# Attention scores on two 64-row halves of the PE array, into two banks, with one query copy

## Chip, cores and metric

The kernel runs on one core of a Trainium2 chip. The metric is the device time of one execution in microseconds (us), as the median of several executions. PE is TensorE, DVE is VectorE, ACT is ScalarE, POOL is GpSimd, SP is SyncE.

## The reference

The input is one sequence of 2048 tokens with 128 features. A first block (a gated linear recurrence with layer norms) is followed by two layers of local attention and a gated feed-forward network. Of one layer the part that matters here is the attention: 8 heads of 64 features, windows of 64 tokens, each query looking at its own window and the one before.

```python
q, k, v = split(shift_token(x) @ wqkv)           # (8 heads, N, 64)
q, k = rotary_xpos(l2norm(q) * qs, l2norm(k) * ks)
bk, bv = look_around(bk), look_around(bv)        # this window and the one before
sim = einsum('bhwid,bhwjd->bhwij', bq, bk)       # 64 queries x 128 keys
sim = where((i < j) | (i > j + WINDOW) | (j == -1), -max, sim)
out = einsum('bhwij,bhwjd->bhwid', softmax(sim), bv)
x = x + out @ wo                                 # then the feed-forward part
```

## The kernel before

**Tiles and groups.** Both layers together are 32 tiles of 128 tokens (two windows each), four tiles to a group. Every engine has its own program, written as `body(G, layer)` over a group with four steps j = 0 to 3; a step works on several tiles at different stages. The order on each engine is written out by hand, and engines wait for each other by semaphores alone. A loop runs the middle groups of each layer.

**One step on PE**, in order: `project_qkv` of tile t (L544, L545, L548: nine products of 512 columns), `project_out` of tile t-4 (L639), `transpose_probs` of tile t-2 (L633), `transpose_qk` of tile t-1 (L604, eight records into two banks), `transpose_o` of tile t-3 (L611), `mix_values` of tile t-2 (L669), and `scores` of tile t-1 (L650 and L655). In the step j = 0 four transposes of the next group's inputs (L595) stand ahead of the scores. In the step j = 2 four transposes of the normalised attention output (L676) stand ahead of the scores, and the feed-forward part of the group before (L544, L545, L548 with `w1`, then L704) behind them. Its third product, L548, waits for `h2_lo`, which DVE writes at L1097 from what ACT wrote at L869.

**One tile on POOL**: the two rotary additions into `rot` (L502, L503), a table (L469), the norms (L479, and L481, a power), in the step j = 1 also the deviations of the group's norm (L486, L488), and the scaling of `rot` (L517). The first needs `kt_done`, the end of the transposes L604 of the tile before, since there is one `rot`; those transposes need `rot_scaled`, the end of L517. So POOL and PE form a loop through `rot`.

**One tile on ACT**: the exponentials (L819), the copy of v (L836), the squares (L840), `probs_t` (L844), then the query copies: heads 0, 2, 4, 6 lie on partitions 0 to 63 of the transposed bank and go to `q_even` (L851), heads 1, 3, 5, 7 on partitions 64 to 127 and go to `q_odd` (L852). The other halves of both tensors are zeros, written once by POOL. Then comes the key copy `k_t` (L856), which PE waits for ahead of the scores, and `o_t` (L861).

**Scores.** A half of the heads (four) goes to one PSUM bank. The mask is a product of a 128 x 128 identity in bf16 with a mask of 512 columns, and each head adds two products with 128 contraction rows (of which 64 meet zeros), 64 stationary columns and 128 moving columns, one for each window. DVE takes the negative maximum of each half (L1081), ACT the exponentials.

Of the kernel before, what the change touches and what calls it, by code (L numbers as in the profile page):

```python
# [11 lines left out]
ALU = mybir.AluOpType  # L12
# [3 lines left out]
P = 128  # L16
DIM = 128
N = 2048
HEADS, DH, WINDOW = 8, 64, 64
# [38 lines left out]
def constant_block():  # L58

    r, c = np.arange(P)[:, None], np.arange(P)[None, :]  # L60
    a = r % WINDOW
    band = (c >= a) & (c <= a + WINDOW)
    first = band & ((r >= WINDOW) | (c >= WINDOW))
    m = lambda ok: np.where(ok, 0.0, MASKED)
    return np.concatenate([np.eye(P), m(band), m(first)], axis=1).astype(np.float32)


def sandwich_kernel(nc, x, w_hg_t, w_out_t, wqkv, wo, ln_g, ln_b, w1, b1, w2, b2,
                    tables, head_scales, consts, out):
    ctx = ExitStack()  # L70
    with ctx:
# [68 lines left out]
        q_even = sb("q_even", [P, PAIRS, P])  # L140
        q_odd = sb("q_odd", [P, PAIRS, P])
# [79 lines left out]
        settled = {e.name: sem(f"settled_{e.name}") for e in (mybir.EngineType.SP, mybir.EngineType.DVE, mybir.EngineType.Pool)}  # L221
# [213 lines left out]
        def _(pool):  # L435
            pool.memset(zeros[:, :], 0.0).then_inc(zeros_ready, 1)
            pool.memset(q_even[:, :, :], 0.0).then_inc(init_done, 1)
            pool.memset(q_odd[:, :, :], 0.0).then_inc(init_done, 1)
# [51 lines left out]
            pool.wait_ge(init_done, 7)  # L490
# [49 lines left out]
        def _(pe):  # L540
# [102 lines left out]
            def scores(a, half):  # L643


                if half == 0 and a.slot == 0:
                    pe.wait_ge(k_carried, a.group + 1)
                need(pe, (pt_saved0, pt_saved1)[half], a.t)
                b = s_bank[half]
                pe.matmul(b[:, :], ident_bf[:, :], mask_bf[1 if a.first else 0][:, :], start=True, stop=True)  # L650
                for h in range(4 * half, 4 * half + 4):
                    q, col = (q_even, q_odd)[h % 2][:, h // 2, :], (h % 4) * P
                    keys = k_t[:, h // 2, a.slot * P:]
                    for low in (0, 64):
                        last = pe.matmul(b[low:low + 64, col:col + P], q[:, low:low + 64], keys[:, low:low + P],  # L655
                                         start=False, stop=True, skip_group_check=True)
                last.then_inc(s_done, 1)

            def mix_values(a):
# [6 lines left out]
                for h in range(HEADS):  # L666
                    cols = slice(h * DH, (h + 1) * DH)
                    for low, v in ((0, v_mid[a.slot]), (64, v_tok[a.slot])):
                        last = pe.matmul(o_bank[low:low + 64, cols], probs_t[:, h, low:low + 64], v[:, cols],  # L669
                                         start=True, stop=True)  # L670
# [38 lines left out]
            pe.wait_ge(init_done, 7)  # L709
# [6 lines left out]
            def body(G, layer):  # L716
# [4 lines left out]
                for j in range(GT):  # L721
# [17 lines left out]
                    if prev.valid:  # L739
                        pe.wait_ge(q_saved, 2 * (prev.t + 1))  # L740
                        pe.wait_ge(k_saved, prev.t + 1)
# [4 lines left out]
                    if prev.valid:  # L746
                        scores(prev, 0)
                        scores(prev, 1)
# [8 lines left out]
        def _(act):  # L757
# [65 lines left out]
            def body(G, layer):  # L823
                number = isinstance(G, int)
                for j in range(GT):
# [22 lines left out]
                    if prev.valid:  # L848
                        act.wait_ge(qt_done, prev.t + 1)
                        need(act, s_done, 2 * prev.t)  # L850
                        act.copy(q_even[0:64, :, :], qt_bank[0:64, :].rearrange("p (c t) -> p c t", c=PAIRS)).then_inc(q_saved, 1)  # L851
                        act.copy(q_odd[64:128, :, :], qt_bank[64:128, :].rearrange("p (c t) -> p c t", c=PAIRS)).then_inc(q_saved, 1)  # L852
# [27 lines left out]
        def _(dve):  # L880
# [206 lines left out]
            def divide_o(a):  # L1087
# [3 lines left out]
                dve.tensor_tensor(o_tok[:, :].rearrange("p (h d) -> p h d", h=HEADS),  # L1091
                                  o_bank[:, :].rearrange("p (h d) -> p h d", h=HEADS),
                                  inv_sum[:, :].unsqueeze(2).broadcast_to([P, HEADS, DH]), ALU.mult).then_inc(o_ready, 1)
# [115 lines left out]
```

## Time and profile before

| | |
|---|---|
| median of 3 runs | 498.43 us (496.94 to 498.90) |
| the profiled execution | 496.46 us, its span 494.70 us |
| PE busy | 393.1 us (79%) |
| PE weight loads busy | 320.7 us (65%) |
| DVE busy | 325.1 us (66%) |
| ACT busy | 309.8 us (63%) |
| POOL busy | 307.1 us (62%) |
| mean granted TensorE clock | 0.923 of full speed |

The span is the stretch from the first to the last instruction; 1.76 us of the execution's time lie around it. Busy shares are means over stages with different limits. Matmuls are pipelined, and their ends in the profile are modelled, so starts tell more than ends. An fp32 product shows as two records in the profile.

### The profile page before, as it was taken

To read this page: it belongs to the slowest core of one execution; us is meant where nothing else is said; L and a number is where in the kernel's file an instruction comes from. 1 tells how busy PE (TensorE), PEld (TensorE's weight loads), DVE (VectorE), ACT (ScalarE), POOL (GpSimd) and SP (SyncE) were. 2 spreads that over 40 slices of the span, in tenths; PEclk is the share of its full clock that TensorE was granted. 3 is DMA by queue.
4 is the path that set the end of the run, shared out by engine and by line. 5 is a ranking of instruction groups with operands and counts; after the bars stand their busy time and mean duration, and the time that the engine had idled before them with its cause. 6 is when DMAs were issued, how large, how long until landed. Compare 5 with 4: busy or idle time off the path is not lost.

```text
span 494.7 us, 11132 instructions
## 1 busy us (share of the span) xinstructions
PE 393.1 (79%) x3768; PEld 320.7 (65%) x3768; DVE 325.1 (66%) x739; ACT 309.8 (63%) x884; POOL 307.1 (62%) x249
## 2 busy tenths in 40 slices
PE   3540058899999999999999989998968999587552
PEld 1330036778787887788878878887857778475432
DVE  6888962757776767766766775777556766545433
ACT  2363065778787787786868877887736867465120
POOL 2016757789889488938893887579574893570021
PEclk9895575999999999999999999999997999799858
DMA  8400240411331052105112410422015111020100
GB/s 300 125 0 0 64 107 1 119 28 28 102 76 30 0 140 57 27 22 139 38 28 52 121 37 19 111 66 52 0 28 143 27 27 27 21 50 1 23 21 21
DMA packets 42398, 28.21 MB, mean 57 GB/s; under 512 B 21699, under 2 KB 36597, under 8 KB 42357
## 3 DMA queue, kind: packets, MB, share of 16 engines
q1 hardware_dynamic: 42357, 27.68, 21.5%
q8 instruction: 23, 0.38, 0.3%
q14 instruction: 18, 0.15, 0.1%
HBM read 13.51 MB, written 3.15 MB: 34 GB/s over the span
## 4 chain that ended last, share of the span: by engine, by line
PE 52%; POOL 22%; DVE 14%; issue 7%; ACT 3%; DMA 1%; POOLq 0%; SPq 0%; DVEq 0%; ACTq 0%
POOL rn L481 8%; PE upper L655 8%; PE bank L544 5%; POOL rot L517 5%; PE bank L548 4%; PE bank L704 4%; PE bank L545 4%; PE bank L669 4%; PE upper L639 4%; PE upper L633 4%; PE bank L604 3%; POOL rot L503 3%; PE upper L604 3%; PE upper L650 2%; POOL tab L469 2%
## 5 line engine op out<-in xcount | busy, mean ns | idle before, releaser
L819 ACT ACTIVATE probs<-upper,neg_max 128x128 f32<-128x128 f32 x256 | 90.4, 368 | 60.7 <-DVE neg_max L1081 60.7
L502 POOL TENSOR_TENSOR rot<-rot_cos,rot_sin 128x512 f32<-128x512 f32 x32 | 40.8, 1275 | 95.4 <-PE upper L604 89.0
L481 POOL TENSOR_TENSOR rn<-floored,minus_half 128x16 f32<-128x16 f32 x32 | 96.7, 3022 | 2.7
L1081 DVE TENSOR_REDUCE neg_max<-upper 128x4 f32<-128x512 f32 x64 | 43.2, 683 | 43.7 <-PE upper L655 43.7
L517 POOL TENSOR_TENSOR rot<-rot,rn 128x1024 f32<-128x1024 f32 x32 | 60.9, 1903 | 1.9
L544 PE MATMUL bank<-wqkv_hi,act_t_hi 128*128 128x512 f32 x96 | 42.8, 446 | 19.9 <-DVE o_tok L1091 12.2
L655 PE MATMUL upper<-k_t,q_even 128*64 128x128 f32 x512 | 54.0, 290 | 0.0
L819 ACT ACTIVATION_READ_ACCUMULATOR probs<-upper,neg_max 128x1 f32 x256 | 52.7, 206 | 0.0
L655 PE MATMUL upper<-k_t,q_odd 128*64 128x128 f32 x512 | 50.7, 277 | 0.0
L1035 DVE TENSOR_TENSOR rot_cos<-bank,tab 128x512 f32<-128x512 f32 x64 | 43.9, 685 | 5.9 <-PE bank L548 5.3
L1035 DVE TENSOR_TENSOR rot_sin<-bank,tab 128x512 f32<-128x512 f32 x64 | 43.5, 680 | 0.0
L1042 DVE TENSOR_REDUCE ss<-sq 128x16 f32<-128x1024 f32 x32 | 38.8, 1211 | 5.7 <-ACT sq L840 5.5
L840 ACT ACTIVATE sq<-bank 128x512 f32<-128x512 f32 x64 | 38.3, 604 | 5.0 <-DVE rot_sin L1035 3.5
L503 POOL TENSOR_TENSOR rot<-rot_cos,rot_sin 128x512 f32<-128x512 f32 x32 | 40.5, 1267 | 0.0
L655 PEld LDWEIGHTS upper<-k_t,q_even 128*64 128x64 f32 x512 | 29.4, 138 | 16.3 <-issue 16.3
L545 PE MATMUL bank<-wqkv_hi,act_t_lo 128*128 128x512 f32 x96 | 39.0, 407 | 0.0
L548 PE MATMUL bank<-wqkv_lo,act_t_hi 128*128 128x512 f32 x96 | 38.9, 406 | 0.0
L669 PE MATMUL bank<-v_mid,probs_t 128*64 128x64 f32 x512 | 36.6, 225 | 1.3 <-ACT probs_t L844 0.9
L544 PEld LDWEIGHTS bank<-wqkv_hi,act_t_hi 128*128 128x128 f32 x96 | 18.8, 195 | 28.9 <-issue 19.6
L639 PEld LDWEIGHTS upper<-wo_sb,o_t 128*128 128x128 f32 x256 | 35.0, 200 | 3.8 <-ACT o_t L861 0.9
L669 PEld LDWEIGHTS bank<-v_mid,probs_t 128*64 128x64 f32 x512 | 32.2, 138 | 6.9 <-issue 5.6
L669 PE MATMUL bank<-v_tok,probs_t 128*64 128x64 f32 x512 | 36.6, 225 | 0.0
(132 smaller groups left out, 970.0 us busy)
## 6 DMA issues: line engine op xcount, KB each, us to landing
v_mid<-v_tok SPq DMA_DIRECT2D x64, 128.0 KB, 2.3
tab_raw<-tables SPq DMA_DIRECT2D x8, 512.0 KB, 3.4
h_tok<-group_in SPq DMA_DIRECT2D x14, 128.0 KB, 3.6
x_res<-group_in SPq DMA_DIRECT2D x28, 64.0 KB, 1.8
wqkv_raw<-wqkv SPq DMA_DIRECT2D x2, 768.0 KB, 6.0
x_in<-x SPq DMA_DIRECT2D x4, 256.0 KB, 3.5
head_scale<-head_scales SPq DMA_DIRECT2D x8, 128.0 KB, 3.9
group_in<-normed SPq DMA_DIRECT2D x4, 256.0 KB
```

The costliest lines, as they stand in the source:

```text
L481: pool.tensor_tensor(rn[:, 0:2 * HEADS], floored[:, 0:2 * HEADS], minus_half[:, :], ALU.pow).then_inc(rn_ready, 1)
L503: pool.tensor_tensor(rot[:, :, 32:64], rot_cos[:, :, 32:64], rot_sin[:, :, 0:32], ALU.add).then_inc(rot_added, 1)
L517: pool.tensor_tensor(rot[:, :, :], rot[:, :, :], rn[:, 0:2 * HEADS].unsqueeze(2).broadcast_to([P, 2 * HEADS, DH]), ALU.mult).then_inc(rot_ ...
L544: pe.matmul(out_ap, lhs, rhs, start=True, stop=False)
L545: pe.matmul(out_ap, lhs_lo, rhs, start=False, stop=False)
L548: return pe.matmul(out_ap, lhs, rhs_lo, start=False, stop=True)
L639: last = pe.matmul(misc_bank[:, 0:DIM], o_t[:, c, :], wo_sb[a.layer][:, c, :], start=(c == 0), stop=(c == 3))
L655: last = pe.matmul(b[low:low + 64, col:col + P], q[:, low:low + 64], keys[:, low:low + P], start=False, stop=True, skip_group_check=True)
L669: last = pe.matmul(o_bank[low:low + 64, cols], probs_t[:, h, low:low + 64], v[:, cols], start=True, stop=True)
L819: last = act.activation(probs[:, h, :], s_bank[half][:, (h % 4) * P:(h % 4 + 1) * P], ACT.Exp, bias=neg_max[a.par][:, h:h + 1], accum_out= ...
L1035: dve.tensor_tensor(dst[:, n * HEADS:(n + 1) * HEADS, :], src, table.unsqueeze(1).broadcast_to([P, HEADS, DH]), ALU.mult).then_inc(done, 1)
L1081: dve.tensor_reduce(neg_max[a.par][:, 4 * half:4 * half + 4], src, AX.X, ALU.max, negate=True).then_inc(max_ready, 1)
```

## The change

Query and key of a head now meet on the 64 partitions on which the head already lies. There is one query tensor, `q_t`, filled by one copy of 128 partitions. Even heads use the array's rows 0 to 63 and write bank 0, odd heads use rows 64 to 127 and write bank 1. The mask comes as four products of a 64 x 64 identity in bf16 with 512 columns, in the same quarters as the scores, ahead of all scores; the mask for a layer's first tile is used for its first window alone. Both halves are issued interleaved in one call, which first waits for both copies out of the two banks, then increments a semaphore. The order of the heads in the two banks changes with it (0, 2, 4, 6 and 1, 3, 5, 7), and so do the columns in `mix_values` and in `divide_o`. Two memsets on POOL at the start fall away.

```diff
-    first = band & ((r >= WINDOW) | (c >= WINDOW))
+    first = band & (c >= WINDOW)
...
-        q_even = sb("q_even", [P, PAIRS, P])
-        q_odd = sb("q_odd", [P, PAIRS, P])
+        q_t = sb("q_t", [P, PAIRS, P])
...
-            pool.memset(q_even[:, :, :], 0.0).then_inc(init_done, 1)
-            pool.memset(q_odd[:, :, :], 0.0).then_inc(init_done, 1)
...
-            def scores(a, half):
-                if half == 0 and a.slot == 0:
+            def scores(a):
+                if a.slot == 0:
                     pe.wait_ge(k_carried, a.group + 1)
-                need(pe, (pt_saved0, pt_saved1)[half], a.t)
-                b = s_bank[half]
-                pe.matmul(b[:, :], ident_bf[:, :], mask_bf[1 if a.first else 0][:, :], start=True, stop=True)
-                for h in range(4 * half, 4 * half + 4):
-                    q, col = (q_even, q_odd)[h % 2][:, h // 2, :], (h % 4) * P
-                    keys = k_t[:, h // 2, a.slot * P:]
+                need(pe, pt_saved0, a.t)
+                need(pe, pt_saved1, a.t)
+                settle(pe)
+                for low in (0, 64):
+                    for half in range(2):
+                        rows = slice(64 * half, 64 * half + 64)
+                        pe.matmul(s_bank[half][low:low + 64, :], ident_bf[rows, rows],
+                                  mask_bf[1 if a.first and low == 0 else 0][rows, :], start=True, stop=True)
+                for p in range(PAIRS):
                     for low in (0, 64):
-                        last = pe.matmul(b[low:low + 64, col:col + P], q[:, low:low + 64], keys[:, low:low + P],
-                                         start=False, stop=True, skip_group_check=True)
-                last.then_inc(s_done, 1)
+                        for half in range(2):
+                            rows = slice(64 * half, 64 * half + 64)
+                            at = a.slot * P + low
+                            last = pe.matmul(s_bank[half][low:low + 64, p * P:(p + 1) * P], q_t[rows, p, low:low + 64],
+                                             k_t[rows, p, at:at + P], start=False, stop=True, skip_group_check=True)
+                            if p == PAIRS - 1 and low == 64:
+                                last.then_inc(s_done, 1)
...
                 for h in range(HEADS):
-                    cols = slice(h * DH, (h + 1) * DH)
+                    head = 2 * (h % PAIRS) + h // PAIRS
+                    cols = slice(head * DH, (head + 1) * DH)
...
-                        scores(prev, 0)
-                        scores(prev, 1)
+                        scores(prev)
...
-                        act.copy(q_even[0:64, :, :], qt_bank[0:64, :].rearrange("p (c t) -> p c t", c=PAIRS)).then_inc(q_saved, 1)
-                        act.copy(q_odd[64:128, :, :], qt_bank[64:128, :].rearrange("p (c t) -> p c t", c=PAIRS)).then_inc(q_saved, 1)
+                        act.copy(q_t[:, :, :], qt_bank[:, :].rearrange("p (c t) -> p c t", c=PAIRS)).then_inc(q_saved, 1)
...
-                dve.tensor_tensor(o_tok[:, :].rearrange("p (h d) -> p h d", h=HEADS),
-                                  o_bank[:, :].rearrange("p (h d) -> p h d", h=HEADS),
-                                  inv_sum[:, :].unsqueeze(2).broadcast_to([P, HEADS, DH]), ALU.mult).then_inc(o_ready, 1)
+                split = lambda ap: ap.rearrange("p (c f d) -> p f c d", f=2, d=DH)
+                inverse = inv_sum[:, :].rearrange("p (f c) -> p f c", f=2).unsqueeze(3).broadcast_to([P, 2, PAIRS, DH])
+                dve.tensor_tensor(split(o_tok[:, :]), split(o_bank[:, :]), inverse, ALU.mult).then_inc(o_ready, 1)
```

## Rows read from the trace of the kernel before

**Rows 1.** The page's first part: busy time, share of the span, instructions.
```profile
PE 393.1 (79%) x3768; PEld 320.7 (65%) x3768; DVE 325.1 (66%) x739; ACT 309.8 (63%) x884; POOL 307.1 (62%) x249
```
**Rows 2.** Waits over the span: waiting group, released by, us, times, longest.
```profile
POOL rot L502 <- PE upper L604: 89.0, 31, 7.6
```
**Rows 3.** Timeline of POOL: start, duration, instruction, idle time before with its releaser.
```profile
157.49 1.28 POOL L502 TENSOR_TENSOR rot<-rot_cos,rot_sin 128x512 f32<-128x512 f32 x1 [0.98 <-PE upper L604]
...
173.98 1.27 POOL L502 TENSOR_TENSOR rot<-rot_cos,rot_sin 128x512 f32<-128x512 f32 x1 [7.57 <-PE upper L604]
...
183.60 1.27 POOL L502 TENSOR_TENSOR rot<-rot_cos,rot_sin 128x512 f32<-128x512 f32 x1 [1.23 <-PE upper L604]
...
193.38 1.28 POOL L502 TENSOR_TENSOR rot<-rot_cos,rot_sin 128x512 f32<-128x512 f32 x1 [1.40 <-PE upper L604]
...
201.00 1.90 POOL L517 TENSOR_TENSOR rot<-rot,rn 128x1024 f32<-128x1024 f32 x1
...
204.22 1.28 POOL L502 TENSOR_TENSOR rot<-rot_cos,rot_sin 128x512 f32<-128x512 f32 x1 [0.98 <-PE upper L604]
```
**Rows 4.** Timeline of PE and ACT around the step j = 1.
```profile
193.60 0.27 PE L669 MATMUL bank<-v_mid,probs_t 128*64 128x64 f32 x1
...
194.50 0.58 ACT L856 COPY k_t<-upper 128x512 f32<-128x512 f32 x1
...
194.53 0.22 PE L669 MATMUL bank<-v_tok,probs_t 128*64 128x64 f32 x1
...
197.87 0.50 PE L544 MATMUL bank<-wqkv_hi,act_t_hi 128*128 128x512 f32 x1
...
200.93 1.04 PE L633 MATMUL upper<-const,probs 128*128 128x128 f32 x8
202.96 0.66 PE L604 MATMUL bank<-const,rot 128*128 128x128 f32 x4 [0.99 <-POOL rot L517]
```
**Rows 5.** Timeline of PE and DVE in the step j = 2.
```profile
206.01 0.38 PE L650 MATMUL upper<-mask_bf,ident_bf 128*128 128x512 bf16 x1
...
207.34 0.39 PE L650 MATMUL upper<-mask_bf,ident_bf 128*128 128x512 bf16 x1
...
207.69 0.69 DVE L1097 TENSOR_TENSOR h_lo<-h_t,h_hi 128x512 fp32r<-128x512 f32 x1 [2.73 <-ACT h_t L869]
...
208.15 0.39 PE L655 MATMUL upper<-k_t,q_even 128*64 128x128 f32 x4
...
208.37 0.39 PE L655 MATMUL upper<-k_t,q_odd 128*64 128x128 f32 x4
...
208.69 0.50 PE L544 MATMUL bank<-h_hi,w_hi 128*128 128x512 f32 x1
...
209.26 0.39 PE L548 MATMUL bank<-h_lo,w_hi 128*128 128x512 f32 x1
```
**Rows 6.** Timeline of POOL over the first tiles.
```profile
77.55 1.26 POOL L502 TENSOR_TENSOR rot<-rot_cos,rot_sin 128x512 f32<-128x512 f32 x1 [2.20 <-PE upper L604]
83.34 1.90 POOL L517 TENSOR_TENSOR rot<-rot,rn 128x1024 f32<-128x1024 f32 x1
88.08 1.28 POOL L502 TENSOR_TENSOR rot<-rot_cos,rot_sin 128x512 f32<-128x512 f32 x1 [2.84 <-PE upper L604]
...
117.44 1.27 POOL L502 TENSOR_TENSOR rot<-rot_cos,rot_sin 128x512 f32<-128x512 f32 x1 [0.98 <-PE upper L604]
```
**Rows 7.** Timeline of PE: restarts after idle time.
```profile
14.60 0.66 PE L554 MATMUL bank<-const,normed 128*128 128x128 f32 x4 [1.74 <-DVE normed L947]
...
75.41 1.12 PE L604 MATMUL bank<-const,rot 128*128 128x128 f32 x4 [4.28 <-POOL rot L517]
...
372.86 0.79 PE L544 MATMUL bank<-wqkv_hi,act_t_hi 128*128 128x512 f32 x1 [6.07 <-DVE o_tok L1091]
```
**Rows 8.** Windows: length, busy us by engine, granted clock, DMA share, GB/s.
```profile
16.00:18.00 2.00, 1.98 (x5) 1.46 (x6) 2.00 (x7) 0.00 (x0) 0.00 (x0) 0.54 0.57 127
18.00:20.00 2.00, 0.83 (x2) 0.11 (x1) 1.97 (x5) 0.00 (x0) 0.00 (x0) 0.60 0.49 116
```

More of the change, by code:

```diff
@@ L220, in sandwich_kernel @@
         dve_chain = sem("dve_chain")
-        settled = {e.name: sem(f"settled_{e.name}") for e in (mybir.EngineType.SP, mybir.EngineType.DVE, mybir.EngineType.Pool)}
+        settled = {e.name: sem(f"settled_{e.name}") for e in (mybir.EngineType.SP, mybir.EngineType.DVE, mybir.EngineType.Pool, mybir.EngineType.PE)}
         block = ctx.enter_context(nc.Block())
@@ L488, in deviation_roots @@
                 pool.tensor_tensor(rn[:, 2 * HEADS:], floored[:, 2 * HEADS:], minus_half[:, 0:GT], ALU.pow).then_inc(done, 1)
-            pool.wait_ge(init_done, 7)
+            pool.wait_ge(init_done, 5)
             def body(G, layer):
@@ L707, in feed_forward @@
                 last.then_inc(down_done, 1)
-            pe.wait_ge(init_done, 7)
+            pe.wait_ge(init_done, 5)
             pe.wait_ge(const_bf, 3)
@@ L739, in body @@
                     if prev.valid:
-                        pe.wait_ge(q_saved, 2 * (prev.t + 1))
+                        pe.wait_ge(q_saved, prev.t + 1)
                         pe.wait_ge(k_saved, prev.t + 1)
```

## Prediction

> **What bounds the kernel now.** I read the page first: PE leads with 79% of the span [rows 1], but no engine is near full, so a share does not say what PE time is worth. The waits say more: POOL's first addition L502 waits 31 times for the transposes L604, 89.0 us in all [rows 2]. That is the loop through the single `rot`: L604 of one tile frees it, POOL adds, takes the power and scales, L517 releases the next L604. So I laid POOL's timeline over a group, since the distance from one L502 to the next is the period of a step [rows 3]. The four are 16.49 us (157.49 to 173.98, the step with the feed-forward part), 9.62, 9.78 and 10.84 us. POOL idles 7.57 us ahead of the first and 1.23, 1.40 and 0.98 us ahead of the others.
>
> The idle 1.2 to 1.4 us is no slack. In the last of the steps L517 ends at 202.90 [rows 3], L604 starts at 202.96 [rows 4], and L502 follows at 204.22 [rows 3]: 1.32 us from scaling to addition are the eight transposes and the hand-overs. So POOL's loop, not PE's work, sets 9.62 and 10.84 us. PE is nearly as late in the two short steps and 0.99 us early in the last [rows 4]. Only the long step is PE's from end to end. Pattern and sizes repeat for six groups. The score work falls once into the long step, and three times into steps in which POOL sets the end.
>
> **The cost of a score call, before.** In the long step it runs from the first mask at 206.01 over the second at 207.34 to the product behind it at 208.69: 1.33 + 1.35 = 2.68 us [rows 5]. Four records (two pairs, both windows at once) are 0.22 us apart (208.15 to 208.37), so a half's sixteen take 0.88. A mask has 512 columns in one pass, as many as two such pairs: 0.22. What is left of 1.33, about 0.24, goes to the two changes between a full-array product and 64-column ones.
>
> **After.** The 16 logical products (32 records) remain. If the row halves overlap, eight slots of 0.11 give 0.88. The nearest row for the rate of issue is L669: 32 records of 64 columns start between 193.60 and 194.53 [rows 4], 0.030 us each, so 0.96 for 32. I take 0.93. The four masks overlap to 0.22 to 0.25. One change of mode in and one out, 0.12 each. Together 1.42 us, 1.26 less. If the row halves do not overlap, it is 0.44 + 1.76 + 0.24 = 2.44, only 0.24 less (the changes of mode saved); the trace of before has no product on half the rows, so both ends stay in the range. I take overlap, because the pairs of column halves, the nearest thing that the trace has, do overlap fully.
>
> The Trainium skill, "TensorEngine Tiling (Array Packing)", Theoretical Speedup and Key Properties, says that a contraction of 64 or less gains up to 2x from row tiling, and that a change of mode drains the array. By that rule the call is the 1.42 us above, without it 2.44. The gaps of 0.1 us at each change in this trace (208.37 + 0.22 to 208.69, [rows 5]) agree with the drain; on the row halves it shows nothing.
>
> The other parts: one query copy for two saves ACT one of about 0.58 us, by the same-sized k copy [rows 4]. In the steps j = 1 that moves `k_t` earlier: it ends at 195.08 while PE's last L669 started at 194.53, so PE gains up to 0.45 us there; the rest of ACT has cover. The strided `divide_o` has the same 512 elements per partition; I set it at nothing (DVE is off the path in all but two steps; if it doubled to 1.4 us it would show in those two, +1.4). The wait for both bank copies costs nothing, since `mix_values` has waited for both already; `settle` is a bare semaphore instruction, hidden by 0.4 us of spare below. Behind the scores PE queues the projection, and DVE and POOL wait for that, with 1 us or more to spare. The first maximum comes after both halves, but both end at 1.42 us, about when the first ended before (1.33). The memsets lie in the start-up, under input loads.
>
> **What of it counts.** (1) The long step, six times. With the scores 1.26 us shorter, L544 starts near 207.4 instead of 208.69. But its third product L548 needs `h_lo`, which DVE ends at 208.38 (207.69 + 0.69), and DVE had waited for ACT, which waited for the transposes ahead of the scores: none of that moves. So L548 goes from 209.26 to about 208.43: 0.83 us, and 0.43 is lost in a new wait [rows 5]. 6 x 0.83 = 5.0 us.
> (2) The first tiles, where PE and ACT are late and the half clock doubles the scores. POOL's loop caps this: from 77.55 a pass takes 7.69 (to the end of L517 at 85.24) plus 1.32, 9.0 us, twice, then 9.65 with the table, twice, which leads to 114.9 instead of 117.44 [rows 6]. PE's own saving there, over 5 us in four calls, is more than the cap. 2.5 us.
> (3) The steps j = 0, 9.78 us against the 9.62 of the pure loop [rows 3]: about 0.1, six times, 0.6 us.
> (4) All other steps: POOL or, in two of the second layer, DVE sets them: 0. The end: 0.
> Sum 8.1 us.
>
> **What it brings with it.** The time won in POOL's steps becomes PE idle time ahead of L604. In the steps j = 1 PE is ready near 201.8 and starts at 202.96. After, it is ready 1.26 + 0.45 = 1.7 us earlier: a gap of about 2.9 us. The granted clock falls to its lower level (1.2 GHz for 2.4) after such gaps in this trace: with idle of 4.28 and 6.07 us each time, and once, near 16 us [rows 8], after a gap of only 1.74 us and one short burst of transposes [rows 7]. The gaps of 1.0 us in six steps never cost it. 2.9 us lies between, so I give each of the six steps near one half. The price: the shortest low stretch with a busy PE is read from two windows, 2 x (1 - 0.54) x 2 + 2 x (1 - 0.60) x 2 = 3.4 us [rows 8], and half of the PE work in it is lost, 1.7 us; right behind this gap follows the long step, in which PE sets the time. With two or three of six: 4.2 us lost. Gaps in the other steps grow to 1.3 to 1.9 us, which I take to hold.
>
> **Forecast.** 8.1 - 4.2 = 3.9 us won. The profiled execution (496.46 us, 494.70 of span and 1.76 around it) would become 492.6; it lies 1.97 us under the median of the runs, 498.43, to which I apply the same difference: 494.5 us, chance 0.38 (two or three falls; own range 493 to 496.5).
>
> **The rivals.**
> - The clock holds, or falls once. For it: no gap under 1.5 us that stood between long busy stretches ever cost it. Against: the event near 16 us [rows 7, 8]. 498.43 - 8.1 = 490.3 (to 492 with one fall). Chance 0.28.
> - Slower by the clock: it falls in four to six steps, or stays low twice as long (as it did for over 5 us after the restart at 75.41). 6 x 1.7 = 10.2, or three at 3.4: 8.1 - 10.2 = +2.1, up to +5: 500.5 to 503; with four falls 497. It turns to a loss from the fifth fall on. Chance 0.16.
> - The row halves do not overlap. Call 2.44 us: 6 x 0.24 = 1.4, the first tiles still some 2.2 from the single copy and the half clock, gap in j = 1 only 1.7 us, so no falls: 3.6 won, 494.8. Chance 0.12.
> - Row halves cost: weight loads and products of the four quarters run one after another, 32 slots of 0.11 = 3.5 us, call 4.2 us. Then each long step is 1.5 longer (9 us) and PE, nearly as late as POOL already, sets the short ones too (some 1.1 in sixteen): +27, 525 us. It decides as soon as a call is longer than 2.68 us. Chance 0.06.
>
> A change of 0.5%, 2.5 us, is about what a measurement of this kernel can tell from none. Faster (under 495.9): 0.28 from the clock that holds, 0.28 of the 0.38, 0.09 of no overlap, 0.65 in all. Same: 0.10, 0.03 and 0.05 from the fourth and fifth fall, 0.18. Slower 0.17. For 8 in 10 the range goes from 490 to 500.5.
>
> **What would show it.** Right: 32 L655 records within about 1 us and four L650 within 0.3; in the long step a new wait of L548 for `h_lo` of some 0.4 us and a period of 15.7 us where the clock holds; the other periods still 9.6 and 10.8; PE idle ahead of L604 in j = 1 near 2.9 us; and dips of the clock right after some of them, with L604 or L669 at double spacing. Wrong: a period of 9.6 that shrinks (then POOL's loop was not the bound), scores as long as before, or a low clock after the 1.3 to 1.9 us gaps as well.

## The result and the profile after

The changed kernel takes 500.76 us (median of 14 runs, 498.48 to 502.21), the kernel before 497.93 us beside it (14 runs, 496.04 to 498.90). The ratio is 1.0061 with a 95% interval of 1.0043 to 1.0079: slower by 3 us. Predicted were 494.5 us, with a range of 490 to 500.5. The profiled execution took 499.41 us with a span of 497.6 us, against 496.46 and 494.70. The line numbers move by two to four in the new file: POOL's addition L499 was L502, L514 was L517; PE's L601 was L604, L630 was L633, L673 was L669, L680 was L676, L541 and L545 were L544 and L548, and L657 are the scores; DVE's L1099 was L1097, ACT's L871 was L869.

The first part of the page of the changed kernel, with the line of the granted clock in 40 slices; it answers to [rows 1]:

```profile
PE 363.8 (73%) x3832; PEld 297.8 (60%) x3832; DVE 329.9 (66%) x739; ACT 287.0 (58%) x852; POOL 304.0 (61%) x247
...
PEclk9995575999999999899989999998998989789957
```

PE has 29 us less to do than before and the kernel is slower. The second line has single eights in its long row of nines, where the kernel before had only nines: the clock falls in places where it held. The windows below show where. The mean granted clock is 0.904 of full speed, against 0.923.

The same wait as [rows 2], among the waits over the span: the bound is still POOL's loop with the transposes.

```profile
POOL rot L499 <- PE upper L601: 91.3, 31, 8.5
```

POOL's timeline over a little more than a group, which answers to [rows 3]:

```profile
155.82 1.28 POOL L499 TENSOR_TENSOR rot<-rot_cos,rot_sin 128x512 f32<-128x512 f32 x1 [0.98 <-PE upper L601]
...
171.58 1.28 POOL L499 TENSOR_TENSOR rot<-rot_cos,rot_sin 128x512 f32<-128x512 f32 x1 [6.85 <-PE upper L601]
...
181.21 1.28 POOL L499 TENSOR_TENSOR rot<-rot_cos,rot_sin 128x512 f32<-128x512 f32 x1 [1.23 <-PE upper L601]
...
190.94 1.28 POOL L499 TENSOR_TENSOR rot<-rot_cos,rot_sin 128x512 f32<-128x512 f32 x1 [1.32 <-PE upper L601]
...
202.63 1.26 POOL L499 TENSOR_TENSOR rot<-rot_cos,rot_sin 128x512 f32<-128x512 f32 x1 [1.80 <-PE upper L601]
...
219.18 1.29 POOL L499 TENSOR_TENSOR rot<-rot_cos,rot_sin 128x512 f32<-128x512 f32 x1 [8.14 <-PE upper L601]
```

The first long step is 15.76 us (155.82 to 171.58), and the short ones behind it 9.63 and 9.73 us. Then comes 11.69 us where 10.87 stood one group earlier, and a long step of 16.55 us. The pair 10.87 + 15.76 = 26.63 us is what the change gives (27.34 before), the pair 11.69 + 16.55 = 28.24 us what it becomes when the clock falls. One of the six pairs is of the first kind, five of the second.

PE's timeline over that second pair, with DVE's subtraction for `h_lo`; it answers to [rows 4, 5]:

```profile
196.90 1.04 PE L630 MATMUL upper<-const,probs 128*128 128x128 f32 x8
...
200.54 1.06 PE L601 MATMUL bank<-const,rot 128*128 128x128 f32 x4 [2.61 <-POOL rot L514]
201.40 1.06 PE L601 MATMUL upper<-const,rot 128*128 128x128 f32 x4
...
205.26 0.41 PE L650 MATMUL upper<-mask_bf,ident_bf 64*64 64x512 bf16 x4
205.50 1.04 PE L657 MATMUL upper<-k_t,q_t 64*64 64x128 f32 x32
206.48 0.50 PE L541 MATMUL bank<-h_hi,w_hi 128*128 128x512 f32 x1
...
206.86 0.69 DVE L1099 TENSOR_TENSOR h_lo<-h_t,h_hi 128x512 fp32r<-128x512 f32 x1 [4.31 <-ACT h_t L871]
...
207.60 0.50 PE L545 MATMUL bank<-h_lo,w_hi 128*128 128x512 f32 x1 [0.39 <-DVE h_lo L1099]
```

The score call runs from 205.26 to 206.48: 1.22 us for what took 2.68. Ahead of the first L601 PE idles 2.61 us, where it idled 0.99. The four records of that L601 take 0.86 us (200.54 to 201.40). Where the clock holds the same row looks like this (PE's timeline, 46 us earlier):

```profile
154.55 0.66 PE L601 MATMUL bank<-const,rot 128*128 128x128 f32 x4 [2.61 <-POOL rot L514]
155.04 0.60 PE L601 MATMUL upper<-const,rot 128*128 128x128 f32 x4
```

There they take 0.49 us, after the same gap of 2.61 us. The windows of the changed kernel (length, busy us by engine, granted clock, DMA share, GB/s) show the low level between 200.7 and 204, and once more near the end:

```profile
200.00:202.00 2.00, 1.46 (x7) 1.46 (x8) 2.00 (x5) 0.36 (x1) 0.83 (x2) 0.66 0.60 131
202.00:204.00 2.00, 2.00 (x21) 1.67 (x21) 0.55 (x1) 1.40 (x3) 1.37 (x2) 0.50 0.00 0
204.00:206.00 2.00, 2.00 (x52) 1.69 (x52) 0.00 (x0) 0.63 (x1) 2.00 (x3) 0.98 0.00 0
...
444.00:446.00 2.00, 2.00 (x27) 1.67 (x27) 0.00 (x0) 1.17 (x2) 0.00 (x0) 0.50 0.00 0
```

**Where 2.9 us of span went.** The table goes by the starts of POOL's L499 (L502 before), as [rows 3, 6] do; it begins with the second of the 32, at which rows 6 begin.

| stretch | before, us | after, us | difference |
|---|---|---|---|
| up to the second addition | 77.55 | 78.22 | +0.7 |
| first tiles, four periods | 39.89 | 37.58 | -2.3 |
| six long steps, each with the step ahead of it, clock held | 27.34 each | 26.63 each | -4.3 |
| falls of the clock in five of these pairs | 0 | 1.4 to 1.6 each | +7.8 |
| all other steps | | | -1.1 |
| behind the last addition | 60.74 | 62.88 | +2.1 |

The start varies by kernel and execution (77.4 to 79.4 us over the profiles of this case), so its 0.7 is not laid on the change. In the row of the other steps nearly all (1.0) comes from the two steps that DVE sets, 17.98 + 17.86 before and 17.52 + 17.31 after. Without filler in these steps their sum lies between 34.5 and 36.8 us over the profiles of this case, and at 34.9 in the kernel before with scores left out for slot 3 (below), so this 1.0 is not laid on the change either. The end: PE idles 0.78 us ahead of the last L601 (at 442.50), the clock falls, and the way to the second L630 of the next step is 1.4 us longer; the rest is a transfer 0.2 us later and a clock that comes back 0.5 us later in the last feed-forward part. The kernel before had no fall at that place.

### The profile page after: what moved, and what is told of

Its sections match the earlier page's. It is cut to its first block, busy times and chain, and to the rows that moved or that the text cites. A ratio compares the mean times of both kernels' runs of the same rounds, so it can differ in the third digit from the quotient of the medians.

```text
span 497.6 us, 11258 instructions
## 1 busy us (share of the span) xinstructions
PE 363.8 (73%) x3832; PEld 297.8 (60%) x3832; DVE 329.9 (66%) x739; ACT 287.0 (58%) x852; POOL 304.0 (61%) x247
## 4 chain that ended last, share of the span: by engine, by line
POOL 34%; PE 32%; DVE 16%; issue 12%; ACT 4%; DMA 1%; POOLq 1%; SPq 0%; DVEq 0%; ACTq 0%
POOL rn L478 14%; POOL rot L514 8%; POOL rot L500 6%; PE bank L708 4%; PE bank L601 4%; PE bank L545 3%; PE upper L601 3%; PE bank L673 3%; POOL tab L466 3%; PE bank L541 3%; PE bank L542 2%; PE upper L636 2%; DVE normed L949 2%; PE upper L608 2%; POOL rot L499 1%
## 5 line engine op out<-in xcount | busy, mean ns | idle before, releaser
L499 POOL TENSOR_TENSOR rot<-rot_cos,rot_sin 128x512 f32<-128x512 f32 x32 | 40.8, 1275 | 97.7 <-PE upper L601 91.3
L478 POOL TENSOR_TENSOR rn<-floored,minus_half 128x16 f32<-128x16 f32 x32 | 94.1, 2940 | 2.7
L541 PE MATMUL bank<-wqkv_hi,act_t_hi 128*128 128x512 f32 x96 | 44.3, 462 | 28.4 <-DVE o_tok L1095 16.0
L514 POOL TENSOR_TENSOR rot<-rot,rn 128x1024 f32<-128x1024 f32 x32 | 60.9, 1904 | 1.9
L601 PE MATMUL bank<-const,rot 128*128 128x128 f32 x128 | 22.5, 303 | 36.6 <-POOL rot L514 36.6
L541 PEld LDWEIGHTS bank<-wqkv_hi,act_t_hi 128*128 128x128 f32 x96 | 18.9, 197 | 43.2 <-issue 31.2
L601 PEld LDWEIGHTS bank<-const,rot 128*128 128x128 f32 x128 | 14.9, 149 | 42.5 <-POOL rot L514 40.3
L673 PE MATMUL bank<-v_mid,probs_t 128*64 128x64 f32 x512 | 39.4, 235 | 0.4 <-issue 0.4
L673 PE MATMUL bank<-v_tok,probs_t 128*64 128x64 f32 x512 | 39.5, 235 | 0.0
L545 PE MATMUL bank<-wqkv_lo,act_t_hi 128*128 128x512 f32 x96 | 39.3, 410 | 0.0
L673 PEld LDWEIGHTS bank<-v_mid,probs_t 128*64 128x64 f32 x512 | 35.1, 148 | 6.9 <-issue 6.7
L630 PE MATMUL upper<-const,probs 128*128 128x128 f32 x256 | 35.1, 278 | 4.9 <-ACT probs L822 4.7
L843 ACT ACTIVATE sq<-bank 128x512 f32<-128x512 f32 x64 | 36.7, 612 | 2.3 <-DVE rot_sin L1037 2.3
```

What stands on the lines that cost most here:

```text
L478: pool.tensor_tensor(rn[:, 0:2 * HEADS], floored[:, 0:2 * HEADS], minus_half[:, :], ALU.pow).then_inc(rn_ready, 1)
L499: pool.tensor_tensor(rot[:, :, 0:32], rot_cos[:, :, 0:32], rot_sin[:, :, 32:64], ALU.add).then_inc(rot_added, 1)
L514: pool.tensor_tensor(rot[:, :, :], rot[:, :, :], rn[:, 0:2 * HEADS].unsqueeze(2).broadcast_to([P, 2 * HEADS, DH]), ALU.mult).then_inc(rot_ ...
L541: pe.matmul(out_ap, lhs, rhs, start=True, stop=False)
L545: return pe.matmul(out_ap, lhs, rhs_lo, start=False, stop=True)
L601: last = pe.transpose(b[:, p * P:(p + 1) * P], rot[:, h:h + 2, :].rearrange("p h d -> p (h d)"), ident)
```

## The experiments

All ratios are to the kernel before, timed in the same batch (497.59, 497.56 and 498.02 us in the three). Three theories stood against each other: **A**, the idle gap of PE ahead of L601 costs the clock, and the falls cost more than the change gives; **B**, products on half the rows are themselves what the clock falls by; **C**, the loss has nothing to do with the clock (the joint wait for both banks, the late first maximum, the new wait for `h_lo`). The gap stands in PE's own step j = 2, the one with the L680 and the feed-forward part; the prediction called it j = 1, after POOL's number for the tile. That slip placed two of the first four kernels at a wrong step, and what they showed is told below.

**The changed kernel once more**, unchanged.

> The changed kernel itself, unchanged, once more. Theory A (gap and clock): the gaps of PE ahead of the qk transposes in the steps j = 1 are 2.6 us and each throws the clock to its lower level by chance, 1.7 us for each fall; the first profile had five falls in six such steps and one more near the end. A second profile should again show four to six of them, not always in the same steps, and a time of 499 to 502 us. Theory B (the half-row products themselves count as less work for the clock, wherever the gap): the same falls, also elsewhere.

Measured 500.12 us (499.90 to 502.39), 1.0065 (1.0048 to 1.0082). The gaps are again 2.60 to 2.62 us (the sixth 2.37), but the falls come in four of the six pairs instead of five, and three more stand elsewhere (one in the first tiles, two in the last steps). Near 16 us the clock is low for 13.7 us, where the kernel before has 3.4 and the first profile nothing. The total repeats, and a single fall does not: the same gap in the same code holds the clock in one group and loses it in the next. The spread of the changed kernel's runs (498.48 to 502.21) is of the size of two or three falls; that it comes from them is not shown, since the kernel before, with no fall in these pairs in its profile, spreads by 2.9 us.

**Filler in the wrong step.** Filler is work whose result nobody reads: eight bf16 products into a bank that the next transposes overwrite, ahead of L601.

```diff
+                        if j == 1:
+                            for _ in range(8):
+                                pe.matmul(kt_bank[:, :], ident_bf[:, :], mask_bf[0][:, :], start=True, stop=True)
                         transpose_qk(prev)
```

> The changed kernel with eight extra mask-shaped products (full array, bf16, 512 columns, 0.22 us each, 1.8 us in all) written into the free k bank ahead of the qk transposes in the steps j = 1; their result is overwritten. They fill the gap of 2.6 us down to 0.8. Theory A: no fall in those six steps, 5 x 1.7 = 8.5 us less than the changed kernel, near 492 us, 6 us under the kernel before; period of the step j = 1 back at 10.85 us and of the long step at 15.75. Theory B (half-row products starve the clock): part of the falls stay, in the long step behind the scores or in the steps j = 3. Rival C (the loss lies in something else, such as the new wait for h_lo): no change or slower by the extra work.

Measured 505.41 us, 1.0180 (1.0151 to 1.0208): a miss, near 492 was expected. PE's timeline of this kernel:

```profile
145.12 1.67 PE L740 MATMUL upper<-mask_bf,ident_bf 128*128 128x512 bf16 x7
...
146.63 0.60 PE L601 MATMUL bank<-const,rot 128*128 128x128 f32 x4
...
157.44 1.03 PE L601 MATMUL bank<-const,rot 128*128 128x128 f32 x4 [2.61 <-POOL rot L514]
```

and POOL's of the same kernel:

```profile
136.80 1.28 POOL L499 TENSOR_TENSOR rot<-rot_cos,rot_sin 128x512 f32<-128x512 f32 x1 [1.23 <-PE upper L601]
...
147.84 1.28 POOL L499 TENSOR_TENSOR rot<-rot_cos,rot_sin 128x512 f32<-128x512 f32 x1 [2.62 <-PE upper L601]
```

The filler (seven of its eight records are in the trace) fills a gap of 0.5 to 0.9 us with 1.7 us of work and delays L601, so POOL's period there is 11.04 us instead of 9.73 (10.36 to 11.04 over the six groups), and in all that adds 5.7 us. The gap of 2.61 us stands untouched in the next step, and three of the six pairs fall; behind the one shown L601 is slow. It tells nothing between A and B, but it gives the price of PE work in a step that POOL sets: nothing up to the gap, most of it beyond.

**The two row halves one after the other.**

```diff
-                for low in (0, 64):
-                    for half in range(2):
-                        rows = slice(64 * half, 64 * half + 64)
+                for half in range(2):
+                    rows = slice(64 * half, 64 * half + 64)
+                    for low in (0, 64):
                         pe.matmul(s_bank[half][low:low + 64, :], ident_bf[rows, rows], ...
-                for p in range(PAIRS):
-                    for low in (0, 64):
-                        for half in range(2):
+                    for p in range(PAIRS):
+                        for low in (0, 64):
```

> The changed kernel with the two row halves issued one after the other: mask and products of half 0, then of half 1; the same 36 products. A call should take 2.3 to 2.45 us instead of 1.22, so the gap in j = 1 shrinks from 2.6 to about 1.5 us. Theory A: no falls or one, the long step 15.75 to 16.3 us, the first tiles still 2 us faster, in all 494 to 495 us: faster than the changed kernel although its scores take twice as long. Theory B: the half-row products are still there and last longer, so the falls stay and the time is over 500 us.

Measured 498.69 us (495.99 to 501.02), 1.0019 (0.9999 to 1.0038): a miss for A, by which 494 to 495 was expected, and under what B said (over 500). It is no measurable difference to before, and with a longer score call it is faster than the changed kernel, whose interval lies above. PE's timeline of one score call:

```profile
159.31 0.40 PE L650 MATMUL upper<-mask_bf,ident_bf 64*64 64x512 bf16 x2
159.55 0.71 PE L655 MATMUL upper<-k_t,q_t 64*64 64x128 f32 x10
160.00 0.40 PE L650 MATMUL upper<-mask_bf,ident_bf 64*64 64x512 bf16 x2
160.09 1.18 PE L655 MATMUL upper<-k_t,q_t 64*64 64x128 f32 x22
161.20 0.50 PE L541 MATMUL bank<-h_hi,w_hi 128*128 128x512 f32 x1
```

The call takes 1.89 us (159.31 to 161.20), not 2.3 or more: half 1's masks start after ten of half 0's sixteen records, so the halves still overlap in part. The gap ahead of L601 shrinks to 2.30 to 2.32 us, yet five of six pairs fall. That profile is of the slowest of the kernel's twelve runs (501.02 us), so the usual number of falls may be smaller. The gap is not the 1.5 us for which A had been put to the test, so the run settles nothing about the clock. What it does show is that a clean long step is 15.78 us, no longer than with 1.22 us of scores, as L545 waits for `h_lo` in any case.

**Less score work in the kernel before, one step early.** Only the last head of each bank in the tiles of slot 2; three quarters of those scores are left out.

```diff
-                for h in range(4 * half, 4 * half + 4):
+                for h in range(4 * half + (3 if a.slot == 2 else 0), 4 * half + 4):
```

> The kernel before with less work: in the steps j = 0 the scores of only one head of four in each bank are computed (the other heads' scores are left out, so the output is not the reference's). All products are on the full 128 rows. That takes 1.3 us from PE once in a group and widens the gap in the step j = 1 from 1.0 to about 2.3 us. Theory A: the clock falls in some of the six steps, 1.7 us each, and the kernel gets slower by 3 to 9 us although it does less. Theory B: no fall, the time of the kernel before, 498 us.

Measured 497.68 us, 1.0004 (0.9992 to 1.0016), where A expected a loss of 3 to 9 us. That is no case against A, for the thinned scores stand one step ahead of the right place: the gap they widen is only 0.38 us, and the one of interest stays (PE's timeline of this kernel):

```profile
191.87 0.66 PE L604 MATMUL bank<-const,rot 128*128 128x128 f32 x4 [0.38 <-POOL rot L517]
...
202.71 0.66 PE L604 MATMUL bank<-const,rot 128*128 128x128 f32 x4 [1.07 <-POOL rot L517]
```

No pair falls, and the time does not move. As a control that holds: three quarters of the scores of eight tiles are worth nothing where POOL sets the step.

**Less score work in the kernel before, in the right step.** The same, for `a.slot == 3`. The products keep all 128 rows, so this is the gap without the half rows.

```diff
+                for h in range(4 * half + (3 if a.slot == 3 else 0), 4 * half + 4):
```

> The kernel before with less work at the right place: for the last tile of each group, whose scores PE computes right ahead of the step with the large gap, only one head of four in each bank is computed (the others' scores are left out, so the output is not the reference's). All products are on the full 128 rows; the gap grows from 1.0 to 2.3 us. Theory A: falls in three to five of the six long steps, 1.7 us each: 503 to 506 us, slower than the kernel before although it does less. Theory B: no falls, 498 us.

Measured 500.94 us (499.02 to 501.68), 1.0058 (1.0036 to 1.0081): the kernel before with work taken out is as slow as the changed kernel, though less slow than A expected (503 to 506). PE's timeline of this kernel:

```profile
157.69 1.12 PE L604 MATMUL bank<-const,rot 128*128 128x128 f32 x4 [2.29 <-POOL rot L517]
```

and POOL's of the same kernel:

```profile
148.12 1.27 POOL L502 TENSOR_TENSOR rot<-rot_cos,rot_sin 128x512 f32<-128x512 f32 x1 [1.40 <-PE upper L604]
...
159.84 1.26 POOL L502 TENSOR_TENSOR rot<-rot_cos,rot_sin 128x512 f32<-128x512 f32 x1 [1.86 <-PE upper L604]
...
177.01 1.27 POOL L502 TENSOR_TENSOR rot<-rot_cos,rot_sin 128x512 f32<-128x512 f32 x1 [8.77 <-PE upper L604]
```

The gap is 2.29 us here (2.29 to 2.41 over the six), and three pairs fall, 11.72 + 17.17 us against 10.84 + 16.50. The gap is enough without the half rows: B is not needed.

**Filler in the right step.** The same eight products in the changed kernel, with `if j == 2`.

> The extra products moved to the right place: the 2.6 us gap stands ahead of the qk transposes in PE's own step j = 2 (the tile whose norms POOL handles in its step j = 1), not in PE's step j = 1, where the first filler only took time. Eight full-array bf16 products of 512 columns, 1.8 us, into the free k bank; the gap falls to 0.8 us. Theory A (the gap costs the clock): no fall in the six long steps, periods 10.87 and 15.76 us in all six groups, 492 to 493 us in all. Theory B (half-row products starve the clock): falls remain around the scores. Theory C (the loss has another cause): no gain, 500 us or more.

Measured 493.75 us (492.58 to 495.72), 0.9932 (0.9906 to 0.9958). PE's timeline:

```profile
152.26 1.67 PE L740 MATMUL upper<-mask_bf,ident_bf 128*128 128x512 bf16 x7
...
154.81 0.66 PE L601 MATMUL bank<-const,rot 128*128 128x128 f32 x4 [0.88 <-POOL rot L514]
```

and POOL's of the same kernel:

```profile
145.21 1.28 POOL L499 TENSOR_TENSOR rot<-rot_cos,rot_sin 128x512 f32<-128x512 f32 x1 [1.32 <-PE upper L601]
...
156.08 1.28 POOL L499 TENSOR_TENSOR rot<-rot_cos,rot_sin 128x512 f32<-128x512 f32 x1 [0.98 <-PE upper L601]
...
171.84 1.27 POOL L499 TENSOR_TENSOR rot<-rot_cos,rot_sin 128x512 f32<-128x512 f32 x1 [6.85 <-PE upper L601]
```

The filler runs in the gap, 0.88 us of it is left, L601 starts no later, and all six pairs are 10.87 + 15.76 us. Products on half the rows are still in every tile, so with this run B falls as the cause by itself. That half rows make a fall more likely at a given gap is not excluded. The new wait of L545 and the joint wait for the banks are also still there, so C falls as well. The falls in the last steps remain (near 442.5 and 449.9 us).

**Half the filler**, `range(4)`.

> The same with four extra products, 0.9 us; the gap is 1.7 us. Theory A: between the gaps that always held (1.0 us) and those that mostly cost the clock (2.3 us): no or one fall, 492 to 494 us. If the clock only needs a gap above about 1.5 us, three or four falls, 497 to 499 us.

Measured 495.02 us (492.89 to 495.37), 0.9939 (0.9918 to 0.9960). PE's timeline:

```profile
155.83 0.65 PE L601 MATMUL bank<-const,rot 128*128 128x128 f32 x4 [1.75 <-POOL rot L514]
```

At gaps of 1.73 to 1.75 us all six pairs are clean.

**Two query copies instead of one** in the changed kernel, as before the change, but into the one `q_t`.

```diff
-                        act.copy(q_t[:, :, :], qt_bank[:, :].rearrange("p (c t) -> p c t", c=PAIRS)).then_inc(q_saved, 1)
+                        act.copy(q_t[0:64, :, :], qt_bank[0:64, :].rearrange("p (c t) -> p c t", c=PAIRS)).then_inc(q_saved, 1)
+                        act.copy(q_t[64:128, :, :], qt_bank[64:128, :].rearrange("p (c t) -> p c t", c=PAIRS)).then_inc(q_saved, 1)
```

> The changed kernel with its one query copy split into two of 64 partitions again, as in the kernel before (into the halves of the same tensor). The key copy ends 0.6 us later, PE waits for it ahead of the scores in the steps without other work there, and the gap shrinks from 2.6 to about 2.2 us. Theory A: falls about as often or one less, and nothing else changes in steady state; 499 to 501 us, equal to the changed kernel within 0.3%. If the single copy brought time of its own, this kernel is slower by more than 2 us.

Measured 498.53 us (497.62 to 503.53), 1.0048 (1.0022 to 1.0075); its interval overlaps with that of the changed kernel. The gap is 2.14 to 2.16 us in four groups and 2.48 to 2.49 in two. Three pairs fall: both with the longer gap, and one of the four with the shorter, behind this row of PE's timeline:

```profile
201.37 0.66 PE L601 MATMUL bank<-const,rot 128*128 128x128 f32 x4 [2.16 <-POOL rot L514]
```

So in four groups 0.45 us of the gap does come from the single copy, as the prediction had it (0.12 in the other two), and a gap of 2.16 us can still cost the clock.

**Two copies with the eight filler products.**

> The changed kernel with the query copied in two parts and the eight extra products in the steps j = 2, to be compared with the same filling and one copy (493.75 us). With the clock held the single copy is worth nothing in the steady state, where POOL's loop sets the end, and up to 0.6 us in each of the first tiles, if PE and ACT set them: 493.7 to 495 us.

Measured 494.43 us (493.25 to 495.93), 0.9932 (0.9916 to 0.9949), the ratio of one copy with the same filler. With the clock held in the six pairs, the single copy is worth nothing that can be measured; the gain lies in the rest of the change, the score call.

**Filler at the end too.** The eight in j = 2, and in the last group 5, 3 and 2 products around `transpose_probs` in the steps j = 1 and 2.

```diff
+                        ending = number and G == LAST - 1 and j in (1, 2)
+                        if ending:
+                            keep_warm(5)
                         transpose_probs(mid, 0)
+                        if ending:
+                            keep_warm(3)
                         transpose_probs(mid, 1)
+                        if ending:
+                            keep_warm(2)
```

> The changed kernel with the eight extra products in the steps j = 2 as before, and more of them (five, three and two, 0.22 us each) around the probability transposes of the last two steps with score work, where the changed kernel showed one or two further falls of the clock after its tile 31 and the kernel before none. Theory A: those falls go as well, 2 to 3 us less than with the eight alone, 491 us. If the end is longer for another reason, such as the wait for both score halves, it stays at 493.7 us.

Measured 492.20 us (491.06 to 493.78), 0.9880 (0.9863 to 0.9897). No fall is left in the last steps, and against the filler in j = 2 alone another 0.5% is gone. The falls at the end cost time as well.

**All of it, and one more place.** The two steps that DVE sets are preceded by 6 us of PE idle [rows 7] and run at the low clock. 26 filler products ahead of the product for v bridge it in the last of them.

```diff
+                        project_qkv(cur, 26 if number and G == LAST - 1 and j == 0 else 0)
```

> The same, and 26 extra products (5.7 us) ahead of the v projection of the last tile, where PE sits idle for 6 to 8 us in both kernels until DVE has divided the output. The six products and sixteen transposes behind that gap then run at the full clock: 1.5 to 2 us less than warm_tail, 489 us; this should be the fastest.

Measured 489.86 us (489.24 to 491.25), 0.9840 (0.9825 to 0.9854), the fastest kernel of this case. POOL's timeline over that step:

```profile
411.83 1.28 POOL L499 TENSOR_TENSOR rot<-rot_cos,rot_sin 128x512 f32<-128x512 f32 x1 [6.84 <-PE upper L601]
...
427.56 1.28 POOL L499 TENSOR_TENSOR rot<-rot_cos,rot_sin 128x512 f32<-128x512 f32 x1 [3.86 <-PE upper L601]
```

It takes 15.73 us, against 17.86 in the kernel before. Falls are left in this profile too: behind the transposes at 86.80 and 125.26 us in the first tiles, and the clock is low around the first of DVE's two steps.

**The same in the kernel before**, with three products in j = 2 in place of eight, as its gap is shorter.

> The kernel before with the same extra products (three instead of eight in the steps j = 2, since its gap there is only 1.0 us). It shows what the filling itself gives without the change. Theory A: the six long steps and the end had no falls to mend, so only the 1.5 to 2 us ahead of the last tile's v projection, 496 us; the change, with the clock held, is then worth 1.3 to 1.6% (7 us).

Measured 498.03 us (496.31 to 500.04), 1.0004 (0.9989 to 1.0018): a miss, 496 was expected. The step that had been 17.86 us is 15.71, so 2.1 us are won there, but they are gone again in a later start, longer first tiles and a longer end (62.3 us behind the last addition, 60.7 without filler). PE's timeline at the end:

```profile
441.74 0.59 PE L632 MATMUL upper<-mask_bf,ident_bf 128*128 128x512 bf16 x2
442.18 0.60 PE L604 MATMUL bank<-const,rot 128*128 128x128 f32 x4
```

There is no idle time left ahead of L604, where the kernel before idled 0.62 us. Of the 1.6 us by which the end is longer, 0.7 is there before the end's first filler (`project_out` starts 4.67 us behind the last addition, for 4.00), and 0.8 comes in the two steps with filler, which is longer than the gaps of this kernel. So the run shows that this filler does not make the kernel before faster. The quotient 489.86 / 498.03 = 0.984 is the change with the same filler at the end in both, but filler laid out for the changed kernel; filler fitted to the kernel before was not tried.

The gaps ahead of L601 (L604 before the change) in the step j = 2, and what followed, one profile each:

| kernel | gap, us | pairs of six with a fall |
|---|---|---|
| before; filler of eight | 1.0 to 1.1; 0.9 | 0; 0 |
| filler of four | 1.73 to 1.75 | 0 |
| two copies | 2.14 to 2.49 | 3 |
| before with less score work | 2.29 to 2.41 | 3 |
| halves apart | 2.30 to 2.32 | 5 |
| filler of eight in the wrong step | 2.59 to 2.62 | 3 |
| changed kernel, twice | 2.60 to 2.62, one 2.37 | 5; 4 |

The table holds for this one place. In the first tiles stands a gap of 1.56 to 1.61 us, near 125 us, in nine profiles of kernels with the change; behind it the clock fell in four of them (the repetition, the filler of four, two copies with filler, all of the filler) and held in five. The changed kernel's two profiles, first PE's timeline of the one that held, then timeline and windows of the repetition:

```profile
124.36 0.63 PE L601 MATMUL bank<-const,rot 128*128 128x128 f32 x4 [1.59 <-POOL rot L514]
```

```profile
125.47 0.68 PE L601 MATMUL bank<-const,rot 128*128 128x128 f32 x4 [1.60 <-POOL rot L514]
...
124.00:126.00 2.00, 0.53 (x5) 0.56 (x6) 1.81 (x2) 1.09 (x3) 1.32 (x1) 0.98 0.50 119
126.00:128.00 2.00, 2.00 (x13) 1.67 (x13) 0.00 (x0) 1.28 (x3) 0.82 (x1) 0.50 0.24 53
```

So the 1.75 us that held six times are no bound below which a gap is safe.

## Why the prediction was wrong

**What bounds the kernel: right.** POOL's loop set the short steps before and sets them now (9.63, 9.73 and 10.87 us where the clock holds, 9.62, 9.78 and 10.84 in [rows 3]), with 29 us less of busy PE. Less score work at a single such step moved nothing (1.0004).

**The score call: right, a little dear.** 1.22 us against the 1.42 taken. The row halves overlap: four masks within 0.24 us and 32 score records within 0.98, at 0.03 us each, the rate of the nearest row, L669. The 0.24 us for two changes of mode don't show as time of their own. The Trainium skill, "TensorEngine Tiling (Array Packing)", Theoretical Speedup, gives up to 2x for a contraction of 64 rows; the trace agrees, with 1.8x for the spacing of the score records (0.055 to 0.031 us). The call as a whole gains 2.2x (2.68 to 1.22), which takes in what the masks and the changes of mode no longer cost. Of the two rivals on the row halves (0.12 and 0.06) neither happened.

**Term (1), the long step: right in mechanism, small error in size.** The wait of L545 for `h_lo` came at 0.39 us (0.43 expected), and a clean long step is 15.76 us, 0.74 less than before for the 0.83 taken. The step ahead of it is 0.03 longer, so the six give 4.3 us for the 5.0 of the sum. That the score call can be 1.89 us without lengthening it shows the cap.

**Term (2), the first tiles: right**, 2.3 us of 2.5.

**Term (3) and the other steps:** the steps j = 0 gave 0.2 us in all instead of 0.6. The two steps of DVE, set at nothing, are 1.0 shorter in this pair of profiles, within what they vary by. The strided `divide_o`, also set at nothing, takes 0.69 us before and after.

**Term (4), the end at nothing: wrong.** In the last steps PE has little left and idles between short bursts. With the scores shorter still, gaps of under 1.3 us were enough: one fall in the profile after and two in its repetition, 1.4 us in the first. That is a mechanism the prediction had, but which it looked for in one place only.

**The step that failed: the number of falls.** Place, length (2.6 us for 2.9) and price (1.4 to 1.6 us each for 1.7) of the gap came out nearly as worked out; the 2.9 took PE as ready near 201.8, where the row's own idle time of 0.99 ahead of 202.96 [rows 4] gives 201.97, and so 2.7. The prediction then gave each of the six "near one half" and took two or three. There were five, and four in the repetition, apart from those at the end and in the first tiles. By the prediction's own sum: 8.1 won and five falls at 1.6 give -0.1, and the end's 2.1 and the start's 0.7 make it +2.7, for 2.9 measured in the span. Against the forecast of 3.9 won, the 6.8 us between are 3.6 for the falls (7.8 for 4.2), 2.1 for the end, 0.7 for the start, and 0.4 of smaller gains. The rival that described this ("it falls in four to six steps", 500.5 to 503 us, chance 0.16) is the one that happened. The evidence used for one half was thin: gaps that held were 1.0 us, gaps that fell 4.28 and more, and the one short gap that fell (1.74 us, [rows 7]) was left out when 2.9 us was placed between the two. The runs now show, at this place, no fall up to 1.75 us, one in four at 2.14 to 2.16, and falls in half of the cases or more from 2.29. The prediction also took the gaps of 1.3 to 1.9 us in the other steps to hold, and named a low clock behind one as a sign of being wrong: they were 0.5 to 1.6 us, and in the repetition one of 1.60 fell.

**What was shown and what not.** That the gap, not the new products, costs the clock is shown twice: made without the new products it costs it, filled with them present it does not. That the falls are what turned a gain into a loss is shown by the filler (0.9932 against 1.0061, same work otherwise), and the value with filler in all these places, 489.86 us, comes near that of the prediction's rival "the clock holds", 490.3. That they agree so well is in part luck: the 2.1 us of the DVE step were not in that sum. What decides between two equal gaps of 2.61 us, one of which holds and the next falls, stays open: no run here separates the time at which the gap comes from what ran before it. The Trainium skill, "Perfetto Trace Analysis", Matmul Optimizations, says that matmuls should be issued back to back in batches, since the engine scales its power with its use. The filler runs agree in direction: 1.7 us of products in each of the six gaps took the ratio from 1.0061 to 0.9932, some 6 us.

## What to carry to other kernels

When another engine's loop sets a step, time saved on PE becomes a PE gap at the point where the two meet, and the clock may fall just ahead of the stretch where PE does set the time; so price the gap together with the saving, at every place where it opens, the drain at the end included. Count the dips of the granted clock in the profile before crediting or blaming the edit itself, and in more than one profile, since the same gap can hold in one and fall in the next. If a gap opens, cheap products into a bank that the next instruction overwrites can bridge it, as long as they end before the awaited semaphore: in a step set by POOL, products that ended about 1 us too late cost 5.7 us over six groups. Filler has to be fitted to the gaps of the kernel at hand: laid out for one kernel, it won nothing in the other.

## What the runs showed of the hardware that had not been expected

- A PE gap of 2.1 to 2.6 us between long busy stretches brought the granted clock to its low level in 23 of 36 cases (the last five rows of the table, with the repetition). It stayed low some 3.4 us of busy PE.
- Whether it falls is not fixed by the code: 5 and 4 of 6 in two profiles of the same kernel, at gaps of which eleven are equal to 0.02 us; in the second, two gaps of 2.61 and 2.37 us held.
- A much shorter gap can be enough elsewhere: at one place in the first tiles, the clock fell behind gaps of 1.56 to 1.61 us in four of nine profiles, with the clock at its full level and PE busy ahead of the gap.
- Row halves overlap even where the instructions of one stand behind all of the other's: half 1's masks started after ten of half 0's sixteen records, and the call took 1.89 us, against 1.22 interleaved.
- The 32 fp32 records on quarters of the array (64 rows, 64 columns, 128 moving columns) start 0.031 us apart, as fast as the records of L669 with all rows and half the moving columns [rows 4], where the score records before stood 0.055 us apart [rows 5].
